# Probabilities as the moving operand, values as a 32-column stationary per column group, and softmax sums spread by a product, in three attention stages

## What is computed

```python
q, k, v = (x projected, split in 16 heads of 8)
att = jnp.einsum('bhqd,bhkd->bhqk', q, k) * (1.0 / np.sqrt(HD))
att = jnp.where(mask, att, -jnp.inf)
att = jax.nn.softmax(att, axis=-1)
y = jnp.einsum('bhqk,bhkd->bhqd', att, v)
y = y.transpose(0, 2, 1, 3).reshape(Bsz, Tlen, Cdim)
return y @ w_proj.T + b_proj        # then added to x
```

## Time and profile before

| | us |
|---|---|
| median of 2 runs | 3782.11 (3780.61 to 3783.62) |
| the profiled execution | 3772.72 |
| its span, first to last instruction | 3771.0 |
| TensorE (PE) busy in the span | 3240.6 (86%) |
| VectorE (DVE) busy | 1380.3 (37%) |
| ScalarE (ACT) busy | 781.5 (21%) |
| GpSimd (POOL) busy | 264.5 (7%) |
| mean granted TensorE clock | 0.724 of full |

### The profile page before, as it was taken

The page is one execution under the profiler, slowest core; times in us unless marked ns, Lnnn a source line. Parts: engine busy times, 40 slices in busy tenths (PEclk is TensorE's granted clock), DMA queues, the critical chain, the costliest instruction groups (busy, mean ns, idle before and its releaser), DMA issues. The chain is left out here.

```text
span 3771.0 us, 46453 instructions
## 1 busy us (share of the span) xinstructions
PE 3240.6 (86%) x15756; PEld 2523.9 (67%) x15756; DVE 1380.3 (37%) x3571; ACT 781.5 (21%) x1430; POOL 264.5 (7%) x359
## 2 busy tenths in 40 slices
PE   5999989999778898965896999994699589898599
PEld 2666656676568787833796566663698367676488
DVE  4333233333143525222222433313333355555344
ACT  1111111111122323222232011112233112121222
POOL 3110011110000100000000210100000000000000
PEclk7555555555589999955898555557799589888699
DMA  3000000000000000000002000000000000000000
GB/s 93 1 1 1 0 0 1 1 1 0 0 1 0 0 0 0 1 0 0 0 0 82 1 1 1 1 1 0 0 0 0 0 9 3 6 3 3 1 0 11
DMA packets 20016, 20.86 MB, mean 6 GB/s; under 512 B 2664, under 2 KB 15184, under 8 KB 19920
## 3 DMA queue, kind: packets, MB, share of 16 engines
q1 hardware_dynamic: 19920, 19.59, 1.6%
HBM read 18.54 MB, written 1.05 MB: 5 GB/s over the span
## 5 line engine op out<-in xcount | busy, mean ns | idle before, releaser
L1031 PE MATMUL L0x_psS<-L0x_km,L0x_qT 32*128 32x512 f32 x192 | 186.0, 1110 | 2.1 <-POOL L0x_km L953 1.4
L1031 PE MATMUL L0a_psS<-L0a_km,L0a_qT 32*128 32x512 f32 x192 | 184.2, 1110 | 3.7 <-DVE L0a_mx_part L1273 1.6
L1031 PE MATMUL L2a_psS<-L2a_km,L2a_qT 32*128 32x512 f32 x192 | 182.1, 1096 | 2.0 <-DVE L2a_mx_part L1273 1.3
L566 PE MATMUL L3x_bank<-L3x_hT,L3x_kTm 128*128 128x256 f32 x512 | 168.7, 427 | 7.6 <-DVE neg_max L836 7.6
L588 PE MATMUL L1a_bank<-L1a_qT,L1a_kTm 128*128 128x256 f32 (+1 forms) x512 | 142.5, 360 | 11.7 <-issue 9.9
L744 ACT ACTIVATE L3x_probs<-L3x_msum 128x512 f32<-128x512 f32 x128 | 80.6, 630 | 339.1 <-DVE L3x_msum L844 339.1
L844 DVE TENSOR_TENSOR L3x_msum<-L3x_bank,L3x_mcol 128x512 f32<-128x512 f32 x128 | 88.5, 692 | 160.3 <-PE L3x_bank L570 160.3
L566 PE MATMUL L1a_bank<-L1a_qT,L1a_kTm 128*128 128x256 f32 (+1 forms) x512 | 108.9, 378 | 37.2 <-DVE scores_L_experts_L L807 35.9
L1813 PEld LDWEIGHTS L2f_psY<-scores_L_experts_L,L2f_hidden 128*128 128x128 f32 x1024 | 133.9, 192 | 8.9 <-issue 2.6
L1827 PE MATMUL L2f_psG<-hT,scores_L_experts_L 128*128 x512 | 132.3, 384 | 6.5 <-ACTq L43 6.5
L553 PE MATMUL L3x_bank<-L3x_kTm,L3x_hT 128*128 128x256 f32 x512 | 135.9, 423 | 0.0
(11 more groups left out here) (635 smaller groups left out, 7063.3 us busy)
## 6 DMA issues: line engine op xcount, KB each, us to landing
experts_L_L<-in_L_ffn_w_dram SPq DMA_DIRECT2D x1, 2048.0 KB, 8.6
scores_L_experts_L<-in_L_ffn_w_dram SPq DMA_DIRECT2D x1, 2048.0 KB, 8.0
L3x_mrow<-in_mask_Bx1xSxS_ff_dram SPq DMA_DIRECT2D x8, 256.0 KB, 2.7
experts_L_L<-n_L_ffn_expert_gate_dram SPq DMA_DIRECT2D x1, 1024.0 KB, 13.4
experts_L_L<-in_L_ffn_expert_up_dram SPq DMA_DIRECT2D x1, 1024.0 KB, 6.9
out_dram<-x_resid SPq DMA_DIRECT2D x1, 1024.0 KB
rope_cos_sin<-in_rope_dram SPq DMA_DIRECT2D x1, 256.0 KB
nat_w_attn<-in_L_attn_w_attn_dram SPq DMA_DIRECT2D x1, 192.0 KB
```

The source lines that it names most:

```text
L566: last = nc.tensor.matmul(at, kTm[:, g, t * P:(t + 1) * P], qT[:, FIRST[t]:S], start=True, stop=stick, skip_group_check=True)
L1031: nc.tensor.matmul(psS[i % 2][:], qT[rows, b % 3, t * P:(t + 1) * P], km[rows, b % 3, :, u * P:(u + 1) * P], start=True, stop=True).then_i ...
```

## The change

In the three stages, `weigh` swaps its operands. The stationary operand is now a window of 32 columns of `v`, and the probabilities stream: 256 query columns for the early keys (t = 0) and 128 for the late ones (t = 1), eight matmuls for a group instead of twelve. Head j writes the 32 PSUM partitions from 32j, that is, uses the array's column group j. `v` gets a slot of 36 columns a head, eight values, a one and zeros; for odd r the window begins 16 columns earlier, so that the groups r = 0 and 1 (and 2 and 3) are summed into the same 32 partitions, in the halves of 16. The result is already transposed: features on the partitions, queries along the free axis, in two halves `a` of 256 columns, with zero rows between.

`divide` changes accordingly: ScalarE copies the result to `raw` (128x512), TensorE's `spread_sums` multiplies with a constant matrix that puts each head's sum on the head's 16 rows (it takes the place of `turn_y`), ScalarE makes the reciprocal as exp(-log), VectorE multiplies into `yT`. `project` sums two products a tile, with weights `wo_rows` whose rows are placed to fit (made once a stage by `out_rows` from a constant `place`). `divide` moves from r = 0 to r = 1 on VectorE; ScalarE's copy stands at r = 0. The product has the same values otherwise.

```diff
@@ load_and_turn, GpSimd
+                steps.step(nc.gpsimd.memset(w["place"][:], 0.0))
+                for a in range(2):
+                    for r in range(2):
...
+                steps.step(nc.gpsimd.memset(w["spread"][:], 0.0))
...
@@ quad_heads, GpSimd
-                nc.gpsimd.memset(v[:], 1.0).then_inc(consts, 1)
+                nc.gpsimd.memset(v[:], 0.0).then_inc(consts, 1)
                 nc.gpsimd.memset(mx[:], 0.0).then_inc(consts, 1)
+                pool.wait_ge(consts, 2)
+                for i in range(3):
+                    at = v[:, i, :].rearrange("p (g e) -> p g e", e=SLOT)
+                    nc.gpsimd.memset(at[:, :, HD:VW], 1.0).then_inc(consts, 1)
@@ TensorE
+                def out_rows():
+                    for a in range(2):
+                        last = nc.tensor.matmul(psN[:, (a + 1) * P:(a + 2) * P], w["place"][:, a, :], wo, start=True, stop=True)
+                    last.then_inc(s_bias, 1)
...
                     if r == 0 and b >= 1:
-                        pe.wait_ge(s_y, b)
-                    for j in range(4):
-                        g = 4 * r + j
-                        first = probs[:, r % 2, j // 2, (j % 2) * S:(j % 2) * S + S]
-                        low = probs[:, r % 2, 2, j * P:(j + 1) * P]
-                        nc.tensor.matmul(O[:, 0, g, :], first[:, 0:P], v[:, b % 3, 0, g, :], start=True, stop=True)
-                        nc.tensor.matmul(O[:, 1, g, :], first[:, P:S], v[:, b % 3, 0, g, :], start=True, stop=False)
-                        last = nc.tensor.matmul(O[:, 1, g, :], low, v[:, b % 3, 1, g, :], start=False, stop=True)
+                        pe.wait_ge(s_raw, b)
+                    a, odd = divmod(r, 2)
+                    for t in range(TPB):
+                        for j in range(4):
+                            g = 4 * r + j
+                            at = (t * H + g) * SLOT - 16 * odd
+                            rows = slice(32 * j, 32 * j + 32)
+                            if t == 0:
+                                nc.tensor.matmul(O[rows, a, :], v[:, b % 3, at:at + 32],
+                                                 probs[:, r % 2, j // 2, (j % 2) * S:(j % 2) * S + S],
+                                                 start=odd == 0, stop=False, skip_group_check=True)
+                            else:
+                                last = nc.tensor.matmul(O[rows, a, P:S], v[:, b % 3, at:at + 32],
+                                                        probs[:, r % 2, 2, j * P:(j + 1) * P],
+                                                        start=False, stop=odd == 1, skip_group_check=True)
                     last.then_inc(s_pv, 1)
...
-                def turn_y(b):
-                    pe.wait_ge(s_y, b + 1)
+                def spread_sums(b):
+                    pe.wait_ge(s_raw, b + 1)
                     pe.wait_ge(s_nm, min(b + 2, B))
-                    for t in range(TPB):
-                        last = nc.tensor.transpose(psN[:, t * P:(t + 1) * P], y[:, t, :], mem.ident[:])
-                    last.then_inc(s_yt, 1)
+                    if b >= 1:
+                        pe.wait_ge(s_x, b)
+                    nc.tensor.matmul(psN[:], w["spread"][:], raw[:], start=True, stop=True).then_inc(s_den, 1)
 
                 def project(b):
                     pe.wait_ge(s_yT, b + 1)
                     for t in range(TPB):
-                        last = nc.tensor.matmul(psN[:, t * P:(t + 1) * P], yT[:, t * P:(t + 1) * P], wo, start=True, stop=True)
+                        for a in range(2):
+                            last = nc.tensor.matmul(psN[:, t * P:(t + 1) * P], yT[:, a, t * P:(t + 1) * P], wo_rows[:, a, :],
+                                                    start=a == 0, stop=a == 1)
                     last.then_inc(s_out, 1)
@@ ScalarE
+                def keep_raw(b):
+                    act.wait_ge(s_pv, 4 * (b + 1))
                     if b >= 1:
-                        act.wait_ge(s_out, b)
-                    nc.scalar.copy(yT[:], psN[:, 0:S]).then_inc(s_yT, 1)
+                        act.wait_ge(s_yT, b)
+                    nc.scalar.copy(raw[:], O).then_inc(s_raw, 1)
+
+                def invert(b):
+                    act.wait_ge(s_den, b + 1)
+                    if b >= 1:
+                        act.wait_ge(s_yT, b)
+                    nc.scalar.activation(rec[:], psN[:].rearrange("p (a q) -> p a q", a=2), ACT.Ln).then_inc(s_ln, 1)
+                    act.wait_ge(s_ln, b + 1)
+                    nc.scalar.activation(rec[:], rec[:], ACT.Exp, scale=-1.0).then_inc(s_rec, 1)
@@ ScalarE, the order
-                        if r == 0 and b + 2 < B:
-                            keep_h(b + 2)
+                        if r == 0:
+                            if b > 0:
+                                keep_raw(b - 1)
+                            if b + 2 < B:
+                                keep_h(b + 2)
                         if r == 1:
                             if b > 0:
-                                keep_y(b - 1)
+                                invert(b - 1)
@@ VectorE
                 def divide(b):
-                    dve.wait_ge(s_pv, 4 * (b + 1))
-                    steps.step(nc.vector.reciprocal(rec[:], O[:, :, :, HD:VW]))
+                    dve.wait_ge(s_rec, b + 1)
                     if b >= 1:
-                        dve.wait_ge(s_yt, b)
-                    nc.vector.tensor_tensor(y[:].rearrange("p t (h e) -> p t h e", h=H), O[:, :, :, 0:HD],
-                                            rec[:].to_broadcast([P, TPB, H, HD]), ALU.mult).then_inc(s_y, 1)
+                        dve.wait_ge(s_out, b)
+                    nc.vector.tensor_tensor(yT[:], raw[:], rec[:], ALU.mult).then_inc(s_yT, 1)
@@ VectorE, the order
-                        if r == 0 and b > 0:
-                            divide(b - 1)
-                        if r == 1 and b + 2 < B and rope:
-                            rotate(b + 2)
+                        if r == 1:
+                            if b > 0:
+                                divide(b - 1)
+                            if b + 2 < B and rope:
+                                rotate(b + 2)
```

More of the change, by code:

```diff
@@ L324, in _ @@
                 steps.step(nc.gpsimd.tensor_copy(w["trinity_f"][:], tri[:]))
+                steps.step(nc.gpsimd.memset(w["place"][:], 0.0))
+                for a in range(2):
+                    for r in range(2):
+                        at = w["place"][:, a, :].rearrange("p (j r e) -> p j r e", j=4, r=2)[:, :, r, 0:HD]
+                        steps.step(nc.gpsimd.affine_select(out=at, in_=at, compare_op=ALU.not_equal, fill=1.0, base=-64 * a - 32 * r,
+                                                           pattern=[[-HD, 4], [-1, HD]], channel_multiplier=1))
+                steps.step(nc.gpsimd.memset(w["spread"][:], 0.0))
+                at = w["spread"][:].rearrange("p (i e) -> p i e", e=16)
+                steps.step(nc.gpsimd.affine_select(out=at, in_=at, compare_op=ALU.not_equal, fill=1.0, base=-HD,
+                                                   pattern=[[-16, 8], [0, 16]], channel_multiplier=1))
                 w["built"] = steps.k
@@ L895, in quad_heads @@
     KINDS = ((0, 0), (1, 0), (1, 1))
-    FILLS = 12
+    FILLS, SLOT = 12, 36
     rope = wq_rot is not None
@@ L915, in quad_heads @@
         turned = sb("roped", [P, 4, S]) if rope else None
-        v = sb("v", [P, 3, TPB, H, VW])
+        v = sb("v", [P, 3, TPB * H * SLOT])
         mx, part = sb("mx", [P, TPB, 4, 32]), sb("mx_part", [P, 2, 4, 4])
@@ L920, in quad_heads @@
         probs = sb("probs", [P, 2, 3, 512])
-        rec, y, yT = sb("rec", [P, TPB, H, 1]), sb("y", [P, TPB, D]), sb("yT", [P, S])
+        raw, rec, yT = sb("raw", [P, 2, S]), sb("rec", [P, 2, S]), sb("yT", [P, 2, S])
+        wo_rows = sb("wo_rows", [P, 2, P])
         out_bias = sb("out_bias", [P, D]) if biased else None
@@ L1009, in values @@
                 def values(b):
-                    if b == 0 and biased:
+                    if b == 0:
                         pe.wait_ge(s_bias_kept, 1)
@@ L1106, in _ @@
                     out_bias_row()
+                out_rows()
                 for b in range(2):
@@ L1148, in _ @@
                             if b > 0:
-                                turn_y(b - 1)
+                                spread_sums(b - 1)
                             if b + 2 < B:
@@ L1162, in _ @@
                 weigh(B - 1, 3)
-                turn_y(B - 1)
+                spread_sums(B - 1)
                 project(B - 1)
@@ L1168, in _ @@
                 act.preload_act_table_set("natural_log_exp_and_others")
+                act.wait_ge(s_bias, 1)
                 if biased:
-                    act.wait_ge(s_bias, 1)
-                    nc.scalar.copy(out_bias[:], psN[:, 0:D]).then_inc(s_bias_kept, 1)
+                    nc.scalar.copy(out_bias[:], psN[:, 0:D])
```

(13 more changed lines are left out.)

14 lines of the change are left out of this document (6 added, 8 removed).

## The result

The changed kernel takes 3220.8 us (median of 2 runs, 3204.1 to 3237.6) against 3782.1 before: ratio 0.852, 95% interval 0.833 to 0.871. Run again beside later experiments it took 3207.9 us, ratio 0.848 (0.844 to 0.852): the median of its three fast runs (3193.5 to 3225.7), without a slow one (3254.7), as the second experiment's figure is without its slow one (3262.2). Predicted were 3210 us and a range of 3080 to 3560. The profiled execution took 3204.1 us, its span 3202.4.

A forecast was written before the change was run, and what follows sets the result against it. PE was taken as the bound, busy 431 of 436 us at a clock of 0.51. Less work and a higher clock save 197 us a stage, 591 in three, less 19 for stage ends: 3782 - 572 = 3210 us, range 3080 to 3560.

The forecast's parts named there:

- Step 1: `weigh` on PE: four column groups overlap fully, 1.7 us in place of 4.98, saving 13.1 us a batch.
- In-order starts: Rival for `weigh`: matmuls start strictly in program order, 3.2 us a `weigh`, 3680 us in all; chance 0.08.
- The clock: PE's clock in the three stages: rises once the thin `weigh` is gone; a high batch takes 0.565 of the low time.
- The likeliest case: Three stages: mostly high clock with full overlap, six of eight batches high, 3210 us (3090 to 3375); chance 0.53.
- the things that would make the prediction fall: Loops of the three stages: clock still 0.5, or its fall coming in the stretch of pairs, now the thinnest.
- The assumed six high batches of eight: Each stage's loop: six batches of 24.8 us and two of 43.0, 235 us in place of 432.
- The high batch: One batch at the high clock: 43.0 x 0.565 = 24.3 us, plus 0.5 for the chain through ACT, 24.8.
- all-high rival: Three stages: all eight batches at the high clock, 683 us saved, 3099 us; no separate chance given.
- Step 2 and 3: `spread_sums` and doubled `project` add 2.1 us a batch on PE; the moved division is covered, 0.5 charged at high clock.
- The wait that the prediction named as the sign: PE idle before L1031 because of DVE: more than 0.5 us a batch would mean the chain through ACT is late.
- Step 4: Stage ends: 3 us more at the start from the larger memset, 3.3 at the end, 19 us in all.
- part 2: PE's added work: `spread_sums` for `turn_y` +1.3 us, doubled `project` +0.85, together +2.1 us a batch.

The follow-up runs named there:

- the second experiment: The changed kernel with the weighted sum's two loops exchanged, so a head's two matmuls stand next to each other: 3211.3 us, ratio 0.849.
- the third group: The changed kernel plus an unused third 32-row matmul beside nearly every pair, and missing last-batch score matmuls issued again: 3099.9 us, ratio 0.819.
- the late wait: The changed kernel with DVE's wait for POOL's memsets moved to the first copy of the values: 3193.3 us, ratio 0.845.
- The widened `weigh`: The kernel before, with each weighted-sum matmul streaming its 9 value columns 14 times over (126 columns): 3247.6 us, ratio 0.859.

## Why the prediction was right

**The sum.** The last batch's division stood at 514.8 in the earlier trace rows and the copy in its place at 325.9: 189 us in L0a. Up to the last one of L2a it is 2538.7 - 1967.5 = 571 us, where the prediction's terms give 591, less three stage starts and two stage ends, 575. For the whole profiled execution it is 3772.7 - 3204.1 = 569 against 572, by the medians 561.

**Step 1, overlap: right.** Four column groups run at once. `weigh` takes 1.44 us, not 1.7: the 0.4 us charged for entering and leaving another division of the array was too much. Above the 1.29 us of streaming there are 0.15 left. The Trainium skill's rule that matmuls start and end in program order ("TensorE: Matmul & The Clock Gate", The mechanism) did not hold: neither the eight passes in 0.85 us nor the order with the heads outermost agree with it. In-order starts would have given 3680 us, far off.

**The clock: right in kind, wrong in its course.** The likeliest case had it rise in the first batch of each stage, hold, and perhaps fall in the last. In L0a it rises only at 121.5, when batch 0 is over; the prediction's reason for the rise was dense work from r=1 to r=3, and `spread_sums` and `project` are issued for the batch before, so batch 0 has neither. It also falls inside the loops, after pairs. This was named among the things that would make the prediction fall, and it did happen (that pairs keep the level had been read from one stretch of 6.8 us): 193 us at a mean of 0.85 hold 58 us at the low clock, of which 27 are the last batch, so 31 us in L0a lie in such falls. The assumed six high batches of eight gave an average of (6 x 24.8 + 2 x 43.0)/8 = 29.4 us; the measured periods are 28.1 to 31.0, and they leave out batch 0. That the total fits (within 4 us by the profiled executions, 11 by the medians) is partly luck: two low batches in each stage were charged, 3 x 2 x (43.0 - 24.8) = 109 us, with only the first and last batches named as places for them. 108 us is what the third group brings back, but only some 50 of them lie at the ends and the rest in falls between.

**The high batch: right.** 24.8 us were worked out; 24.6, 25.4 and 25.8 were measured where the clock stayed high, with the third group's work beside it. The all-high rival of 3099 us is what that kernel took, 3099.9, to within 1 us.

**Step 2 and 3.** At the high clock PE is busy in 162 of 168 us of that kernel's L0a loop; all idle time together is 0.9 us a batch. The wait that the prediction named as the sign, PE's before the score matmuls for DVE, is 1.0 us in that loop and in L0x's and 2.6 in L2a's, 0.1 to 0.4 a batch where 0.5 were charged. DVE's need of 17.5 us a batch is under the period.

**Step 4: right.** The memset takes 2.98 us (3.1 predicted). In the kernel before, the first product came 1.2 us after the memset's start:

```profile
46.48 0.43 DVE L1231 TENSOR_TENSOR L0a_h<-x_resid,mean_var 128x256 f32<-128x256 f32 x1 [4.26 <-POOL L0a_mx L947]
```

The memset stands at 45.31 there. In the changed kernel the product comes 3.7 us after it, so a stage starts 2.5 us later, where 3 were charged, and the late wait brought back about 8 of the 9 us of three stages, a difference not clear of the spread of the runs. At the stage's end the chain grew by 3.9 - 2.0 = 1.9 us and the projection by 0.85, 2.7 in all. The prediction says 3.3, but its own terms add up to 4.8 - 2.7 + 0.85 = 3.0; of the difference to that, `spread_sums` at the high clock explains 0.6 (1.12 us in place of 1.72), and the rest of the chain took a little more than its terms.

**What was mis-sized** is how much of the gain is the clock's. The prediction split 572 us into 245 for less work and 327 for the clock. The widened `weigh`, with all its passes, gives 539 by the clock alone, where the change as a whole gives 577 (3784.6 less 3207.9; each beside its own runs of the kernel before). The two gains are not a sum: at the high clock the overlap is worth 2.59 - 0.79 = 1.8 us a `weigh`, 173 us in 96 of them; part 2 at half its price takes 25 of it and the stages' starts and ends 16, which leaves 132. The changed kernel is only 40 us under the widened one (3207.9, 3247.6), because its loops hold the clock less well, 0.82 to 0.88 against 0.95 to 0.96. With the third group it is 148 under it.

## What to carry to other kernels

Where PE is nearly always busy and its granted clock still stands at half, look for the stretch in which the least of the array is in use (few columns behind each weight load, 32 rows of 128) and fill that first; a moving side that is widened inside the time of its weight load costs next to nothing (2.68 us against 2.59 at the high clock, nothing at the low one). After a change that shortens the step, look again: the thinnest stretch is then another one, and idle row groups can carry work that only keeps the clock. Column groups of four heads overlap as row groups do, whatever the order of the instructions.

## What the runs showed of the hardware

- With the same instructions, the same durations at the low clock (0.43 us a matmul) and PE busy 98 to 99% of the loop in both, 9 moving columns leave the clock at 0.51 and 126 lift it to 0.96. The Trainium skill says that the clock follows how busy PE has been ("TensorE: Matmul & The Clock Gate", What's actually happening). Busy time as the profile counts it does not tell these runs apart; how much of the array streams does.
- Rows count too: the same 1.44 us on 32 rows instead of 128 cost 154 us, and left the loops' clock at 0.65 to 0.68 in place of 0.82 to 0.88.
- What a third row group does for the clock depends on the rest of the step: the loops stand at 0.99 to 1.00 with it where `weigh` is thick, and at 0.51 to 0.54 where `weigh` is thin. Which quantity the chip goes by, and over what stretch, was not settled here.
- Three row groups stream at once: their first passes start within 0.01 us, and a batch at the high clock takes 26.2 us with and without the third.
